# Zero products in TensorE's waits, a product moved from GpSimd to VectorE, and a new order table in the third stretch of a two-layer decoder

## The chip, the cores and the metric

The kernel runs on one core of one Trainium2 chip. The metric is the device time of one execution in microseconds (us); the median of three runs of the kernel before is 1454.74 us (1453.48 to 1459.05). An engine works through its instructions in order; semaphores make it wait for others. TensorE is PE in the rows, VectorE DVE, ScalarE ACT, GpSimd POOL, SyncE SP.

## What is computed

16 sequences of 128 tokens of width 256 go through two layers, in float32. Layer 0 is a gated state-space block, a cross attention and a mixture of 32 experts. Layer 1, the third stretch of the kernel, is

```
x = x + attn(layernorm(x))                 # causal, 16 heads of 16, with an entropy-dependent temperature
x = x + xattn(layernorm(x), ctx)           # one head of 256, plus a bias phi
x = x + ffn(layernorm(x))                  # grouped-query causal attention with rotary positions, then 2 of 8 experts

def adaptive_temperature_softmax(logits):
    p = softmax(logits)
    entropy = sum(-p * log(p + 1e-09))
    e2 = entropy * entropy
    poly = POLY[0]*e2*e2 + POLY[1]*e2*entropy + POLY[2]*e2 + POLY[3]*entropy + POLY[4]
    beta = where(entropy > 0.5, maximum(poly, 1.0), 1.0)
    return softmax(logits * beta)
```

## The kernel before

**Stretches.** Phase A (layer 0's block and cross attention and the choice of experts) ends near 338 us of the span, phase B (32 experts) near 660. `phase_c` is layer 1. It begins near 671 and ends with the tiles of the second mixture of experts (39 tiles of 128 rows, `Tiles`).

**Pairs and units.** `phase_c` works on 8 pairs (`g`) of two sequences. A pair passes through `first` (combine the results of layer 0's experts with x: `comb`; norm; transposes `t0`; projections `q`, `k`, `v`), attention `one` with the temperature, `mix` (`t1`, output projection `o`, cross attention `xk`, `xv`, `xq`, `xs`, `xtr`, `xo`), `rotary` (`t3`, `rk`, `rr`, `rq0`, `rq1`, `rv`), attention `two`, and `last` (`t5`, `o2`, `t6`, `gate`). An attention has four units (`u`: sequence and half of the heads), each of 128 x 1024 elements. For `xk` and `xv`, pairs 0 and 1 compute their context's keys and values here; the others load them.

**A unit of attention one** goes: mask and score products on TensorE (`sc`, L1466, L1468), maximum and subtraction on VectorE (`mx` L1523, `sb` L1529), exponential on ScalarE (`ex`, L1762), sum and reciprocal on VectorE (`zr`, L1779), scaling on GpSimd (`pn`, L1796), logarithm on ScalarE (`ln`, L1767), the product p log p on GpSimd (`pr`, L1799), its sum on VectorE (`hr`, L1784), the polynomial of the entropy on GpSimd (`po`, ten operations of 128 x 8, L1802 to L1817), scaling of the logits on GpSimd (`db`, L1820), second exponential on ScalarE (`e2`, L1556), eight transposes on TensorE (`tr`, L1486), copy on ScalarE (`pt`, L1559), values (`pv`, L1498), copy (`os`, L1563), two transposes (`ot`, L1504), and the division on VectorE (`out`, L1537, L1539). Attention one has one pair of score banks: the next pair's scores of unit u wait for this pair's `pt` of unit u, and the transposes of unit u + 1 wait for the next pair's `sb` of unit u.

**What sets the order.** Each engine's program is woven from generators, each of which says when its next piece is due; the due times stand in the table `AT_C`, one entry for each piece and pair, in us. The table sets only the order in which an engine's instructions are put in its queue; at run time semaphores decide when they run. The pieces of the tiles and of the routing tables (`tables_tensor`, `tables_vector`) hang on entries of it (`t5` and `wta`).

**Fetches.** `fetch0` to `fetch3` of a pair are gathers that GpSimd issues (L2309); `comb` waits for all four, and from pair 2 on, a pair's first fetch waits for `comb` two pairs before. `comb` is L1707, four instructions that read two tiles in SBUF each.

**Zero products.** `keep_warm(c, con, n, bank)` issues n products of zeros, 128 x 128 by 128 x 256, each two matmul instructions in the trace (L1085). There are ten before the third stretch's first wait and five in the first pair's `t0`, two after the second scores.

## Time and profile before

| | us |
|---|---|
| median of three runs | 1454.74 |
| lowest and highest | 1453.48, 1459.05 |
| the profiled execution | 1466.06 |
| its span | 1463.2 |
| busy in the span: TensorE, VectorE, ScalarE, GpSimd | 1312.7, 779.7, 689.0, 536.1 |
| mean granted clock of TensorE, share of full speed | 0.963 |

Shares are means over stages with different limits, so stages are read one by one. Times in rows are us from the span's start. The granted clock of a stretch is given as a share of 2.4 GHz; at 0.50 it is the lower of its two levels, 1.2 GHz. A busy TensorE is not TensorE at its peak, since matmuls overlap and their ends are modelled.

### The profile page before, as it was taken

What the parts mean: (1) busy time and instruction counts of PE and PEld (TensorE: products, weight loads), DVE (VectorE), ACT (ScalarE), POOL (GpSimd) and SP (SyncE); (2) the same over time, 40 slices, a digit from 0 to 9 for tenths busy, and PEclk for the clock granted to TensorE, in tenths of its full rate; (3) what the DMA queues carried; (4) which work ended last, traced back from release to release, by engine and by line L of the source; (5) the groups of instructions that cost most, each with busy time, mean ns of one, the idle gap of its engine ahead of it and who ended that gap; (6) DMA issues with size and microseconds to landing.
All of it is one profiled execution on the core that took longest, in us unless ns stands there. A gap on an engine that the chain in (4) does not pass through costs nothing. (4 is left out here: it accounts for less than half of the span.)

```text
span 1463.2 us, 23121 instructions
## 1 busy us (share of the span) xinstructions
PE 1312.7 (90%) x8464; PEld 989.9 (68%) x8464; DVE 779.7 (53%) x1791; ACT 689.0 (47%) x1254; POOL 536.1 (37%) x777
## 2 busy tenths in 40 slices
PE   9899999988999999896667989989989779999996
PEld 7576767757999999894334665656656545666664
DVE  4876868673111111113656687977776645433332
ACT  6454747552222222222447687768777445222221
POOL 2123130402000000006878887887867033322222
PEclk9999999999999999998869999999999989999998
DMA  9673563903877777713000001000010634322221
GB/s 352 252 200 106 123 166 106 230 12 124 292 264 264 262 267 280 279 48 98 19 1 5 20 29 33 20 29 20 0 48 16 243 97 136 60 39 41 44 39 11
DMA packets 70686, 171.00 MB, mean 117 GB/s; under 512 B 8508, under 2 KB 47425, under 8 KB 60464
## 3 DMA queue, kind: packets, MB, share of 16 engines
q1 hardware_dynamic: 54944, 144.39, 30.9%
q0 software_dynamic: 10224, 16.09, 5.3%
q10 hardware_dynamic: 5408, 9.04, 1.7%
q8 instruction: 69, 1.13, 0.3%
q14 instruction: 41, 0.34, 0.1%
HBM read 123.11 MB, written 48.07 MB: 117 GB/s over the span
## 5 line engine op out<-in xcount | busy, mean ns | idle before, releaser
L1187 ACT ACTIVATE b_ht<-ps,b_b 128x154 f32<-128x154 f32 x256 | 85.4, 387 | 205.8 <-PE ps L1154 189.5
L1202 DVE TENSOR_SCALAR b_yt<-ps,b_b 128x154 f32<-128x154 f32 x64 | 21.2, 373 | 244.0 <-PE ps L1167 244.0
L2309 POOL DMA_INDIRECT experts<-ye,gidx_all x32 | 32.1, 1002 | 325.2 <-SPq L1093 314.6
L2384 PE MATMUL ps<-experts,d_xt 128*128 x312 | 147.1, 594 | 1.2 <-ACT d_xt L2440 0.8
L1154 PE MATMUL ps<-b_xet,ring 128*128 128x154 f32 x1024 | 143.7, 298 | 3.7 <-ACT b_ht L1187 3.7
L1154 PEld LDWEIGHTS ps<-b_xet,ring 128*128 128x128 f32 x1024 | 138.3, 192 | 3.9 <-issue 3.8
L1167 PE MATMUL ps<-b_ht,ring 128*128 128x154 f32 x1024 | 139.7, 294 | 0.4 <-DVE b_yt L1202 0.4
L1167 PEld LDWEIGHTS ps<-b_ht,ring 128*128 128x128 f32 x1024 | 136.3, 189 | 0.6 <-issue 0.6
L2526 POOL DMA_INDIRECT out_dram<-d_yd,d_to x39 | 60.6, 1554 | 158.5 <-DVE d_yd L2498 151.2
L1523 DVE TENSOR_REDUCE c_mx<-ps 128x8 f32<-128x1024 f32 x64 | 77.8, 1215 | 63.8 <-PE ps L1468 63.3
L1486 PE MATMUL ps<-cf,experts 128*128 128x128 f32 x512 | 73.3, 290 | 24.8 <-DVE experts L1529 12.6
L1486 PEld LDWEIGHTS ps<-cf,experts 128*128 128x128 f32 x512 | 61.5, 149 | 37.0 <-ACT experts L1556 18.4
L2384 PEld LDWEIGHTS ps<-experts,d_xt 128*128 128x128 f32 x312 | 56.0, 190 | 41.0 <-issue 39.0
L1799 POOL TENSOR_TENSOR experts<-experts 128x1024 f32<-128x1024 f32 x32 | 75.4, 2360 | 13.3 <-ACT experts L1767 13.3
L1559 ACT ACTIVATE experts<-ps 128x1024 f32<-128x1024 f32 x64 | 65.4, 1023 | 30.7 <-PE ps L1486 26.0
L235 POOL TENSOR_SCALAR a_rs<-a_mv 128x2 f32<-128x2 f32 x24 | 6.0, 250 | 200.3 <-DVE a_mv L190 200.3
L1529 DVE TENSOR_TENSOR experts<-ps,c_mx 128x1024 f32<-128x1024 f32 x64 | 78.1, 1220 | 1.6 <-PE ps L1498 0.2
L1468 PE MATMUL ps<-experts 64*128 64x512 f32 x256 | 78.7, 694 | 0.0
L1556 ACT ACTIVATE experts<-experts 128x1024 f32<-128x1024 f32 x64 | 67.5, 1057 | 22.9 <-DVE experts L1529 13.3
L2402 PE MATMUL ps<-experts,d_gt 128*128 x312 | 73.9, 380 | 0.9 <-DVE d_gt L2479 0.9
L2447 ACT ACTIVATE d_gs<-ps 128x512 f32<-128x512 f32 x39 | 23.3, 597 | 105.4 <-PE ps L2384 102.4
L1796 POOL TENSOR_TENSOR experts<-experts,c_zz 128x1024 f32<-128x1024 f32 x32 | 60.7, 1898 | 14.3 <-DVE c_zz L1781 14.0
(336 smaller groups left out, 2839.0 us busy)
## 6 DMA issues: line engine op xcount, KB each, us to landing
ring<-in_w SPq DMA_DIRECT2D x64, 1024.0 KB, 5.4
xd<-zero SPq DMA_DIRECT2D x6, 3120.0 KB, 25.9
a_kp<-in_ctx_k SPq DMA_DIRECT2D x8, 1024.0 KB
experts<-in_wd SPq DMA_DIRECT2D x1, 7424.0 KB
d_xd<-xd SPq DMA_DIRECT2D x39, 130.0 KB, 2.1
xe<-zero SPq DMA_DIRECT2D x1, 4928.0 KB, 33.2
b_xe<-xe SPq DMA_DIRECT2D x32, 154.0 KB
ye<-b_ye ACTq DMA_DIRECT2D x32, 154.0 KB
```

The costliest lines, as they stand in the source:

```text
L1154: r = pe.matmul(ps[:, b, CAP * (m % 2):CAP * (m % 2) + CAP], w1r[:, slot, k, P * m:P * m + P], xet[:, e % 2, k, :], start=(k == 0), stop=( ...
L1167: r = pe.matmul(ps[:, 5, CAP * j:CAP * j + CAP], w2r[:, slot, m, P * j:P * j + P], ht[:, e % 2, m, :], start=(m == 0), stop=(m == MF0 - 1) ...
L1187: r = a.activation(ht[:, e % 2, m, :], ps[:, b, CAP * (m % 2):CAP * (m % 2) + CAP], ACT.Gelu, bias=b1[:, e, m:m + 1])
L1468: m = pe.matmul(ps[:, b0 + b, :], l.qt[64 * b:64 * b + 64, ch, P * s:P * s + P], l.kp[64 * b:64 * b + 64, ch, :, P * s:P * s + P], start=F ...
L1486: m = pe.transpose(ps[:, there.b0 + h // 4, P * (h % 4):P * (h % 4) + P], d[:, h, :], con["ident"])
L1523: v.tensor_reduce(l.mx[u][:, :], both, AX, ALU.max).then_inc(*c.dv.up())
L1529: v.tensor_tensor(l.d[u % l.n_d][:, :, :], both, l.mx[u][:, :, None].to_broadcast([P, NU, P]), ALU.subtract).then_inc(*l.dd.up())
L1556: a.activation(d[:, :, :], d[:, :, :], ACT.Exp).then_inc(*l.ee.up())
L1559: a.activation(d[:, :, :], l.scores(c, g, u), ACT.Copy).then_inc(*l.pt_in.up())
L1799: pool.tensor_tensor(e, e, l, ALU.mult).then_inc(*pr.up())
L2384: m = pe.matmul(ps[:, b, :], xt[:, j % 2, k, :], w13[:, bass.ds(e, 1), f:f + F1], start=(k == 0), stop=(k == KD - 1))
L2402: m = pe.matmul(ps[:, 4, 0:D], gt[:, j % 2, f, :], w2[:, bass.ds(e, 1), D * f:D * f + D], start=(f == 0), stop=(f == MF1 - 1))
```

## The change

Four things change, all in `phase_c`.

1. Zero products are issued ahead of waits: for attention one ahead of the transposes of all units of pair 0 and unit 0 of pair 1, for pair 1 ahead of `k` and `v`, for attention two ahead of the transposes of unit 2 of pair 6, for pair 7 ahead of `rq0`, and four ahead of the first count of the routing tables. They write banks that are not in use there (5, 0).
2. For pairs 0 and 1 (`BY_VECTOR = 2`) the product p log p is issued on VectorE.
3. The polynomial is computed as a product of two quadratic factors, which are found on the host: nine operations on GpSimd, with five dependent steps.
4. The table `AT_C` is another one throughout. Some of its entries (us, pairs 0 to 7):

| piece | before | after |
|---|---|---|
| fetch0 | 0, 3.8, 11.5, 20.5, 27, 146.6, 157, 202 | 0, 1.3, 11.5, 16.7, 28.4, 32.3, 86.7, 68 |
| fetch3 | 3.7, 8.8, 19.3, 25.7, 34, 158.2, 169.2, 211.7 | 5, 8.8, 19.3, 27.2, 38.7, 46.7, 98.1, 73.7 |
| xk (pairs 0, 1) | 17.2, 131.5 | 3.6, 134.8 |
| xv (pairs 0, 1) | 33.2, 136 | 6.4, 138.3 |
| xvi (pairs 0, 1) | 38.9, 137.9 | 8.3, 140.2 |
| comb | 6.4, 10.2, 20.6, 27.1, 40.1, 176.1, 193.9, 231.6 | 9.5, 12.5, 20.6, 28.6, 62.1, 50.6, 99.5, 80.3 |
| t0 | 12.5, 25.9, 79.5, 122.6, 194, 260.1, 316.6, 378 | 15.2, 27.9, 81.2, 126.2, 196.5, 261.9, 313.2, 372.4 |
| tr0 | 51.6, 86.9, 133.3, 183.6, 243.7, 305.8, 358.9, 418.6 | 48, 88.9, 127, 185.5, 245.7, 303.3, 358.3, 415.8 |
| db0 | 47.9, 81.5, 124.2, 177.2, 234.4, 295.9, 351.3, 408.2 | 44.8, 77.3, 117.9, 178.8, 237.1, 295.3, 350, 403.4 |
| t1 | 82.6, 138.7, 188.4, 244.6, 303.1, 358.4, 415.5, 462.2 | 84.4, 141, 193.1, 245.2, 305.3, 357.8, 415.3, 458 |
| tr2b | 159.6, 215.5, 267.5, 321, 385.1, 443.7, 486.3, 517.9 | 157.8, 216.2, 269.8, 327.9, 381.1, 436.1, 479.4, 517.4 |
| t3 (pair 7) | 487.9 | 485 |
| rq0 (pair 7) | 497.1 | 492.8 |
| t5 | 178.7, 238.1, 299.6, 353.7, 416, 460.1, 504.9, 527 | 179.3, 240.2, 298.3, 352.8, 411.9, 454.2, 497.2, 523.3 |

The code, without the table:

```diff
+BY_VECTOR = 2
+def quadratic_factors(p):
+    roots = sorted(np.roots([p[0], -p[1], p[2], -p[3], p[4]]), key=lambda r: (abs(r.imag), r.real))
+    return [(float(-(r + s).real), float((r * s).real)) for r, s in (roots[:2], roots[2:])]
+FACTORS = quadratic_factors(POLY)
...
         yield at("tr", u)
+        keep_warm(c, con, *warm.get((g, u), (0, 0)))
         pe.wait_ge(*l.ee.at(g, u))
...
             yield at("k")
+            if g == 1:
+                keep_warm(c, con, 4, 5)
             pe.wait_ge(*one.q_in.at(g))
...
             yield at("v")
+            if g == 1:
+                keep_warm(c, con, 5, 5)
             pe.wait_ge(*one.k_in.at(g))
...
                 v.reciprocal(zz[u][:, :], zz[u][:, :]).then_inc(*zr.up())
+                if g < BY_VECTOR:
+                    yield at("pr", u)
+                    v.wait_ge(*ln.at(g, u))
+                    v.tensor_tensor(e[:, :, :], e[:, :, :], lnp[u % 2][:, :, :], ALU.mult).then_inc(*pr.up())
                 yield at("hr", u)
...
-                yield at("pr", u)
-                pool.wait_ge(*ln.at(g, u))
-                pool.tensor_tensor(e, e, l, ALU.mult).then_inc(*pr.up())
+                if g >= BY_VECTOR:
+                    yield at("pr", u)
+                    pool.wait_ge(*ln.at(g, u))
+                    if g == BY_VECTOR and u == 0:
+                        pool.wait_ge(*pr.at(g - 1))
+                    pool.tensor_tensor(e, e, l, ALU.mult).then_inc(*pr.up())
                 yield at("po", u)
                 pool.wait_ge(*hr.at(g, u))
-                pool.tensor_tensor(sq_h, h, h, ALU.mult).then_inc(*c.po.up())
-                pool.tensor_scalar(g_h, h, -0.5, None, ALU.is_lt)
+                pool.tensor_tensor(square, h, h, ALU.mult)
+                pool.tensor_scalar(p, h, *FACTORS[0], ALU.mult, ALU.add)
+                pool.tensor_scalar(other, h, *FACTORS[1], ALU.mult, ALU.add).then_inc(*c.po.up())
+                pool.tensor_scalar(chosen, h, -0.5, POLY[0], ALU.is_lt, ALU.mult)
                 pool.wait_ge(*c.po.now())
-                pool.tensor_scalar(p, sq_h, POLY[0], POLY[2], ALU.mult, ALU.add)
-                pool.tensor_scalar(odd, sq_h, -POLY[1], -POLY[3], ALU.mult, ALU.add).then_inc(*c.po.up())
+                pool.tensor_tensor(p, p, square, ALU.add)
+                pool.tensor_tensor(other, other, square, ALU.add).then_inc(*c.po.up())
                 pool.wait_ge(*c.po.now())
-                pool.tensor_tensor(p, p, sq_h, ALU.mult)
-                pool.tensor_tensor(odd, odd, h, ALU.mult).then_inc(*c.po.up())
+                pool.tensor_tensor(p, p, other, ALU.mult).then_inc(*c.po.up())
                 pool.wait_ge(*c.po.now())
-                pool.tensor_tensor(p, p, odd, ALU.add).then_inc(*c.po.up())
-                pool.wait_ge(*c.po.now())
-                pool.tensor_scalar(p, p, POLY[4], None, ALU.add).then_inc(*c.po.up())
-                pool.wait_ge(*c.po.now())
-                pool.tensor_tensor(p, p, g_h, ALU.mult).then_inc(*c.po.up())
+                pool.tensor_tensor(p, p, chosen, ALU.mult).then_inc(*c.po.up())
                 pool.wait_ge(*c.po.now())
                 pool.tensor_scalar(p, p, 1.0, None, ALU.max).then_inc(*be.up())
...
                 if half == 0:
+                    if g == NG - 1:
+                        keep_warm(c, con, 6, 0)
                     pe.wait_ge(*two.k_in.at(g))
...
+            yield from weave([first_tensor(g), causal_tensor(c, one, con, g, tick(g), True, {(0, 0): (4, 5), (0, 1): (5, 5), (0, 2): (5, 5), (0, 3): (5, 5), (1, 0): (4, 5)}), mix_tensor(g), rotary_tensor(g),
+                              causal_tensor(c, two, con, g, tick_b(g), False, {(NG - 2, 2): (9, 0)}), last_tensor(g)])
...
                 yield settled[n] + LATE * n
+                if n == 0:
+                    keep_warm(c, con, 4, 0)
                 pe.wait_ge(*router.pr_in.at(choice))
```

## Rows read from the trace of the kernel before

**Rows 1.** Windows: span, us, busy time and count by engine, clock, DMA share, GB/s.

```profile
722.00:762.00 40.00, 26.14 (x133) 12.29 (x132) 18.82 (x25) 17.70 (x21) 32.43 (x53) 0.59 0.00 1
762.00:1160.00 398.00, 352.83 (x2587) 239.84 (x2587) 298.12 (x574) 290.54 (x468) 297.66 (x504) 0.98 0.10 34
1160.00:1198.00 38.00, 23.85 (x142) 14.43 (x142) 18.98 (x67) 11.53 (x21) 10.45 (x16) 0.78 0.53 179
1219.00:1449.00 230.00, 228.85 (x874) 141.78 (x874) 91.69 (x271) 53.60 (x128) 65.74 (x47) 1.00 0.29 51
```

**Rows 2.** Timeline of TensorE, last pair: start, us, line, tiles, count, idle before.

```profile
1217.88 0.66 PE L253 MATMUL ps<-cf,experts 128*128 128x128 f32 x4 [0.41 <-DVE experts L1539]
```

**Rows 3.** Windows, the 10 us ahead of the slow stretch.

```profile
710.00:720.00 10.00, 4.03 (x16) 2.20 (x17) 8.60 (x11) 5.54 (x8) 9.15 (x17) 1.00 0.00 0
```

**Rows 4.** Timeline of TensorE, a step at low and at full clock.

```profile
724.32 1.97 PE L1486 MATMUL ps<-cf,experts 128*128 128x128 f32 x8 [2.22 <-ACT experts L1556]
729.37 2.04 PE L1468 MATMUL ps<-experts 64*128 64x512 f32 x4
...
768.55 1.04 PE L1486 MATMUL ps<-cf,experts 128*128 128x128 f32 x8
...
773.76 1.13 PE L1468 MATMUL ps<-experts 64*128 64x512 f32 x4
```

**Rows 5.** Chain of waits, pair 7's first transposes of mix.

```profile
1145.74 0.59 PE ps L253 x4
```

**Rows 6.** Timelines, zero products and start of the third stretch.

```profile
660.13 2.32 PE L1085 MATMUL ps<-zero 128*128 128x256 f32 x10
671.07 9.46 PE L1085 MATMUL ps<-zero 128*128 128x256 f32 x30 [8.61 <-PEq L1093]
680.89 0.66 PE L253 MATMUL ps<-cf,experts 128*128 128x128 f32 x4 [0.36 <-ACT experts L226]
682.24 1.99 PE L272 MATMUL ps<-c_xt_f,weights 128*128 128x256 f32 x8 [0.69 <-ACT c_xt_f L262]
...
671.55 1.80 DVE L1707 SCALAR_TENSOR_TENSOR x_all<-experts,gwt_all,x_all 128x256 f32<-128x256 f32 x4
```

**Rows 7.** Timeline of GpSimd, product and polynomial of one unit.

```profile
731.32 2.35 POOL L1799 TENSOR_TENSOR experts<-experts 128x1024 f32<-128x1024 f32 x1
733.62 0.21 POOL L1802 TENSOR_TENSOR c_sq_h<-c_en 128x8 f32<-128x8 f32 x1
...
736.31 1.90 POOL L1820 TENSOR_TENSOR experts<-experts,c_po 128x1024 f32<-128x1024 f32 x1
```

**Rows 8.** Timelines, a combine beside GpSimd, and the combines' durations in ns.

```profile
698.93 1.91 DVE L1707 SCALAR_TENSOR_TENSOR x_all<-experts,gwt_all,x_all 128x256 f32<-128x256 f32 x1
...
698.31 0.95 POOL L2309 DMA_INDIRECT experts<-ye,gidx_all  x1 [0.30 <-issue]
699.28 1.27 POOL L1749 TENSOR_TENSOR x_all<-x_all,weights 128x512 f32<-128x512 f32 x1
...
L1707 DVE SCALAR_TENSOR_TENSOR x_all<-experts,gwt_all,x_all x32: 472/479/1911, 671.5 to 915.7; 128x256 f32<-128x256 f32 x32
```

**Rows 9.** Timeline of VectorE, a subtraction of 1024 columns.

```profile
733.04 1.21 DVE L1529 TENSOR_TENSOR experts<-ps,c_mx 128x1024 f32<-128x1024 f32 x1
```

**Rows 10.** Waits between 775 and 1146: us, times, longest.

```profile
ACT experts L1556 <- POOL experts L1820: 8.6, 11, 1.7
```

**Rows 11.** Timelines of the last pairs, TensorE and ScalarE.

```profile
1174.00 1.97 PE L1486 MATMUL ps<-cf,experts 128*128 128x128 f32 x8 [5.55 <-ACT experts L1556]
1175.98 1.12 PE L253 MATMUL ps<-cf,c_x_rms 128*128 128x128 f32 x4
...
1188.25 3.78 PE L272 MATMUL ps<-c_xt_r,weights 128*128 128x256 f32 x8 [3.37 <-ACT experts L1574]
...
1185.77 2.42 ACT L1574 ACTIVATE experts<-ps,cf 128x512 f32<-128x512 f32 x4 [2.45 <-PE ps L1968]
```

**Rows 12.** Windows, behind the first zero products.

```profile
680.00:690.00 10.00, 6.90 (x31) 4.94 (x29) 1.57 (x6) 5.13 (x10) 8.71 (x11) 1.00 0.16 43
```

More of the change, by code:

```diff
@@ L1297 @@
 AT_C = {
[87 rows of a table removed]
-    "xadd": (185.7, 244.3, 305.3, 362.1, 425.5, 465.6, 510.8, 531.1), "rtp": (187, 245.6, 306.6, 363.4, 433, 467.3, 513.6, 532.4),
[3 rows of a table removed]
-    "count": (None, 254.6, None, 374.9, None, 476.6, 522.3, 539.6), "gap": (None, 255, None, 372.8, None, 476.7, 522.3, 539.6),
-    "wta": (None, 257.5, None, 376.3, None, 478.1, 522.8, 540.1), "weights": (None, 259.1, None, 379.9, None, 485.5, 524.1, 541.4),
[4 rows of a table removed]
[87 rows of a table added]
+    "xadd": (185, 245.3, 307.4, 359.5, 416.8, 461.5, 501.3, 527.4), "rtp": (186.3, 246.6, 306.4, 358.5, 420.4, 463.2, 502.6, 528.7),
[3 rows of a table added]
+    "gap": (None, 256.3, None, 368.3, None, 472.6, 511.3, 535.8), "count": (None, 256.3, None, 367.5, None, 472.4, 514.1, 535.8),
+    "wta": (None, 259.2, None, 369.9, None, 474, 518.5, 536.3), "weights": (None, 260.8, None, 371.5, None, 481.4, 519.8, 537.6),
[4 rows of a table added]
 }
@@ L1441, in earlier, with causal_tensor @@
     return tally.at(n, j)
-def causal_tensor(c, l, con, g, at, woven):
+def causal_tensor(c, l, con, g, at, woven, warm):
     pe, ps = c.nc.tensor, c.ps
@@ L1608, in phase_c @@
         zz, en, po = ([sb("%s%d" % (name, u), [P, NU]) for u in range(len(UNITS))] for name in ("zz", "en", "po"))
-        gt = [[sb("%s%d" % (name, u), [P, NU]) for name in ("sq_h", "g_h", "odd")] for u in range(len(UNITS))]
+        gt = [[sb("%s%d" % (name, u), [P, NU]) for name in ("square", "other", "chosen")] for u in range(len(UNITS))]
         x_rot, x_rms = [sb("x_rot%d" % n, [P, GS, D]) for n in range(2)], sb("x_rms", [P, GS, D])
@@ L1792, in unit @@
                 e, l, d = ent[u % 2][:, :, :], lnp[u % 2][:, :, :], one.d[u][:, :, :]
-                h, p, (sq_h, g_h, odd) = en[u][:, :], po[u][:, :], (x[:, :] for x in gt[u])
+                h, p, (square, other, chosen) = en[u][:, :], po[u][:, :], (x[:, :] for x in gt[u])
                 yield at("pn", u)
@@ L2161, in tensor_program @@
         def tensor_program(g):
-            yield from weave([first_tensor(g), causal_tensor(c, one, con, g, tick(g), True), mix_tensor(g), rotary_tensor(g),
-                              causal_tensor(c, two, con, g, tick_b(g), False), last_tensor(g)])
+            yield from weave([first_tensor(g), causal_tensor(c, one, con, g, tick(g), True, {(0, 0): (4, 5), (0, 1): (5, 5), (0, 2): (5, 5), (0, 3): (5, 5), (1, 0): (4, 5)}), mix_tensor(g), rotary_tensor(g),
+                              causal_tensor(c, two, con, g, tick_b(g), False, {(NG - 2, 2): (9, 0)}), last_tensor(g)])
         def vector_program(g):
```

188 rows, old and new, of the table AT_C are left out of this document.

## The prediction

> **What bounds the kernel now.** I read the stages first: mean load and granted clock of four stretches [rows 1]. TensorE is busy 229 of 230 us in the last one, where the experts' tiles run back to back, and no edit lies there: it only shifts with the moment at which the last pair's transposes (L253, 1217.88) start [rows 2]. Before that, the reader is to look at the granted clock. It is 0.98 for 398 us in the middle, 0.59 in 722 to 762 (TensorE busy 26 of 40 us) and 0.78 in 1160 to 1198. The slice 710 to 720 says what went ahead: TensorE was busy 4.0 of 10 us, still at clock 1.00, and the clock fell behind it [rows 3]. The level in such a stretch is 1.2 GHz instead of 2.4, and it doubles TensorE's steps: eight transposes take 1.97 us where they take 1.04 at full clock, the score products 2.04 and 1.13 [rows 4].
>
> Then I laid the trace beside the kernel's own due times, as marks along the program, not as prices. The first unit's transposes (`tr0`, pair 0, due 51.6) start at 724.32, so the origin is 672.7; `tr0` of pair 1 (86.9) starts at 768.55 [rows 4], origin 681.7: 9.0 us lost. `t1` of pair 7 (462.2) starts at 1145.74 [rows 5], origin 683.5: only 1.9 us more in 377. `t5` of pair 7 (527.0) at 1217.88 [rows 2], origin 690.9: 7.4 more. So the loss lies where the clock is low, and there the change puts its zero products.
>
> **The change part by part.**
>
> *Start, by hand from rows.* The new order puts `xk`, `xv` and `xvi` ahead of `comb` of pair 0 on TensorE, ScalarE and VectorE. Now VectorE combines pair 0 at 671.55, and TensorE turns it at 680.89 after 30 zero instructions that began at 671.07 [rows 6]. In the new order TensorE first runs its ten zero products (20 instructions; two thirds of the 9.46 us of 30, to about 678), then `xk` 1.99 (the form's row), its bias on ScalarE (two pieces, by half of L1574's four in 2.42: 1.2), `xv` 1.99, `xvi` (half of a 1024-wide VectorE operation of 1.2: 0.6), so `comb` starts at about 683.7, 12 us late. Today pair 0 waits on from 673.4 for GpSimd, which has fetches queued; that slack goes, so `t0` comes near 689.8, 9 us late. Queued behind: GpSimd's first fetch of pair 2 waits for `comb` of pair 0, and with it fetches of pairs 3 to 5. Much is absorbed: pair 0's units are stretched today by GpSimd (products 2.35 us each on it [rows 7]), and four of these go to VectorE. Following both orders row by row I reach `db0` of pair 0 at about 721 in both. But TensorE has the zero products: four ahead of `k`, five ahead of `v`, four ahead of `tr0`. One product is two instructions, and ten instructions took 2.32 us at full clock, 0.46 us per product [rows 6]; at half the clock I double it. Thirteen are 6.0 us, of which some 4 fit in waits. So `tr0` comes 2.0 us **late** (726.3). Bounds: 0 to +9 (nothing absorbed).
>
> *The pairs 0 and 1, from 724.32 to 768.55.* 44.2 us today, four steps. What full clock gives back in a step: 0.93 (transposes), 0.91 (scores), and about half as much again for the mask's and the values' products, which also run in a step (an estimate): 2.6, four times, some 10 us, all between TensorE's wait and VectorE's next, of which 9.0 showed as loss. The zero products (five per step, 2.3 us) sit in front of the transposes, in the wait for VectorE's maximum and subtraction (two of 1.2 us), and are hidden there at full clock; four ahead of `tr0` of pair 1 are not, TensorE being dense in 762 and on: +1.0 after some slack. Against it, the new order has three more combines and twelve fetches in these pairs (1.80 us each for a combine, 0.95 for a fetch on GpSimd [rows 6, 8]), and its own due times make the distance 40.9 where the old made it 35.3. If the clock is held: 44.2 to 40.9 is −3.3; +1.0 for the zeros.
>
> *The product on VectorE.* No row has this operation on VectorE. Nearest are its 1024-wide subtraction and sums, 1.2 us [rows 9]; I take 1.2, bounds 1.2 and 3.1. The upper bound is from the combine, which reads two tiles in SBUF: a piece takes 0.48 us, but the one that began at 698.93 lasted to 700.84 (1.91), and GpSimd's two-input addition ran from 699.28 to 700.55 [rows 8]. A 1.9 us GpSimd operation can hold a product as long. Eight products leave GpSimd (8 × 2.36); +0.8 on the path for one or two collisions. The page "SBUF — State Buffer" of the Trainium skill, section "Who interferes with whom", says it as a rule: a VectorE instruction with two SBUF inputs and a GpSimd one that reads SBUF exclude each other, the later one waiting for the whole of the other. The trace agrees, and the rule speaks against this move: if each of the eight products met half of a scaling, it would give 7.6 us of collisions in place of 0.8, and this part +5 in place of −1.5. So for this part −3.3 + 1.0 + 0.8 = **−1.5** (bounds −9 and +6).
>
> *The polynomial.* Today 2.69 us from L1802 (733.62) to the scaling (736.31), ten small operations in seven dependent steps [rows 7]. New: nine in five. By the same spacings (0.17 independent, 0.29 per dependent step) 2.23: 0.46 less for every unit. It counts where GpSimd is last before ScalarE's second exponential: 11 times between 775 and 1146 [rows 10]. 11 × 0.46 is **−5.0** for the middle. Bounds: 0 (TensorE, 353 of 398 us busy there, takes it back) and −11 (all 24 units). The later fetches and combines that left the middle are counted in it; the due times give −6.2.
>
> *Last pairs.* Three waits carry the loss: 5.55 us ahead of the transposes at 1174.00 (then 1.97), ScalarE's keys 1185.77 to 1188.2 while TensorE stands 3.37, then `rq0` 3.78 us where its form takes 1.99 at full clock [rows 6, 11]. The nine zero products (4.2 us) ahead of `tr2b` of pair 6 fill the first, four ahead of the counts the wait before it, six (2.8 us) ahead of `rq0` the last, 0.5 over the 2.4 us of keys. With clock, `rq0` gives 1.8. The new order puts `t3`, `rk`, `rr` nearer: 12.3 us today from 1175.98 to 1188.25, 7.8 by the new marks plus 0.8 for zeros: −3.7. `t3` itself waits for VectorE, which now does a subtraction first, +0.5; the rest of the pair is 0.6 longer by its marks. Sum −1.8 − 3.7 + 0.5 + 0.5 = **−4.5** (bounds −8 and 0).
>
> Sum: +2.0 − 1.5 − 5.0 − 4.5 = **−9.0 us**, from a span of 1463.2 to 1454. The profiled execution took 1466.06 with what lies around its span, 11 us over the median of the runs (1454.74); I take the difference over unchanged: **1446 us**.
>
> **Rivals.**
> *A, forecast*: clock held in most waits, 1441 to 1450; 0.42.
> *B, clock held throughout.* All 16.4 us of origin drift in the two slow stretches go but 3, and the middle gives its 5: 1454.7 − 13 − 5 = 1437. For it: the drift lies so squarely there. Against: the loaded start, and waits such as those behind pair 1 that get no zeros. 0.20.
> *C, no net change.* The start and collisions eat the early gain and the middle is TensorE's: +2 + 1.5 − 1.5 − 4.5, about 1452. For it: TensorE 353 of 398 in the middle. 0.30. That includes the case that zero products do not lift the clock; but in 680 to 690, behind the zero stretch, the clock was 1.00 with TensorE busy 6.9 of 10 us [rows 12], which speaks against.
> *D, slower.* The zero products meet the clock already low, which the late start makes likely (VectorE's chain leaves TensorE waiting 3 to 4 us before `sc3`). At 1.2 GHz five take about 4.6 us in a wait of 2.4, +2 in each of four steps; the thirteen ahead of `k`, `v`, `tr0` take 5 more, those ahead of `tr0` of pair 1 one more. +2 + 8 + 5 + 1 − 5.0 − 4.5 is about +7, 1462; it decides once fewer than half of the early waits run at full clock. Against: a low clock ends behind dense work. 0.08.
>
> **How the numbers follow.** A measurement tells 0.5% (7.3 us) from no change. Faster by more (below 1447.5): most of A and B, 0.55. Within: part of A and C, 0.37. Slower: D, 0.08. The range leaves out some of B's and D's far ends: 1437 to 1456.
>
> **What would show it.** Granted clock in the 40 us behind the first transposes: near 1.0 for A and B, 0.6 for D. `comb` of pair 0 starting near 684 and `t0` near 690 show the start; `tr0` of pair 0 near 726 its absorption. VectorE's product at 1.2 us, or up to 3.1 where GpSimd runs. The chain from L1802's successor to the scaling 2.2 us. Clock 1.00 around the end's transposes and `rq0` 2 us long. From the last `t5` to the end 245 us as now. I am wrong if the first transposes come before 722 or behind 731, if the middle (`tr0` of pair 1 to `t1` of pair 7, 377 us) does not shrink, or if the early clock stays at 0.6.

## The result: no gain, and where the expected one went

The changed kernel takes 1464.22 us (median of 18 runs, 1458.34 to 1470.05), the kernel before 1460.47 beside it (18 runs, 1453.48 to 1464.72): ratio 1.0033, 95% interval 1.0020 to 1.0046. A later set of runs has it at 0.9994 (0.9969 to 1.0019). It is the same within the 0.5% that a measurement can tell; the forecast was 1446 us, 0.6% below before, with a range of 1437 to 1456.

A warning for all that follows: the median of the kernel before moved between sets of runs, from 1459.3 to 1469.7 us, and single profiled executions of one kernel differ by 3 to 8 us. So I compare ratios and times within a set and name the set; ratios of different sets are compared only with this in mind. Traces serve for where time goes, not for how much.

The same windows of the kernel after as in [rows 1], and then the 20 us behind its start, in this execution and in a second one of the same kernel (columns as there: busy time of TensorE, weight load, VectorE, ScalarE, GpSimd, then the granted clock):

```profile
722.00:762.00 40.00, 28.20 (x173) 17.30 (x173) 29.83 (x43) 19.08 (x24) 35.92 (x60) 0.87 0.07 20
762.00:1160.00 398.00, 353.27 (x2596) 242.27 (x2628) 302.70 (x584) 291.01 (x470) 281.24 (x463) 0.97 0.10 34
1160.00:1198.00 38.00, 32.32 (x177) 22.78 (x178) 19.16 (x59) 13.57 (x27) 12.62 (x19) 0.87 0.46 151
1219.00:1449.00 230.00, 228.31 (x875) 141.70 (x874) 92.08 (x271) 52.46 (x127) 65.01 (x46) 1.00 0.28 50
684.00:704.00 20.00, 13.60 (x43) 8.67 (x44) 10.29 (x26) 5.68 (x10) 15.24 (x22) 0.83 0.16 47
```

```profile
684.00:704.00 20.00, 12.34 (x32) 8.00 (x30) 7.80 (x21) 4.60 (x9) 11.52 (x16) 0.66 0.16 47
722.00:762.00 40.00, 31.30 (x168) 20.55 (x167) 32.71 (x42) 19.18 (x23) 33.41 (x56) 0.87 0.07 20
```

The zero products did lift the clock: 0.87 in 722 to 762 instead of 0.59. What they did not do is save time there. TensorE's timeline of after gives the marks that answer to [rows 2, 4, 5]:

```profile
671.61 6.68 PE L1095 MATMUL ps<-zero 128*128 128x256 f32 x20 [8.70 <-PEq L1103]
...
726.42 0.82 PE L1497 MATMUL ps<-cf,experts 128*128 128x128 f32 x6
...
770.98 1.89 PE L1095 MATMUL ps<-zero 128*128 128x256 f32 x8
772.70 1.04 PE L1497 MATMUL ps<-cf,experts 128*128 128x128 f32 x8
...
1142.49 0.66 PE L263 MATMUL ps<-cf,experts 128*128 128x128 f32 x4
...
1216.71 0.66 PE L263 MATMUL ps<-cf,experts 128*128 128x128 f32 x4 [0.41 <-DVE experts L1550]
```

The first transposes of pair 0 come at 726.42 (I had 726.3), those of pair 1 at 772.70 where before had 768.55. From these rows, and the same four marks in every later kernel, I divide the stretch into four parts: *start* (first zero product of the third stretch to `tr0` of pair 0), *pairs 0 and 1* (to `tr0` of pair 1), *middle* (to `t1` of pair 7) and *end* (to `t5` of pair 7). All in us, one profiled execution each:

| kernel | start | pairs 0 and 1 | middle | end |
|---|---|---|---|---|
| before | 53.2 | 44.2 | 377.2 | 72.1 |
| after | 54.8 | 46.3 | 369.8 | 74.2 |
| after, second execution | 62.1 | 45.6 | 370.7 | 71.7 |
| old order, all other edits | 55.1 | 35.6 | 374.6 | 72.8 |
| the same, second execution | 55.4 | 35.6 | 371.9 | 69.5 |

The third and fourth line are the answer in short, and the experiments below lead to it. Line numbers: the changed file is 10 to 24 lines longer there, so L1497 is the transposes, L1570 their copy, L1567 the second exponential, L1822 or L1801 the product (GpSimd or VectorE), L1840 the scaling of the logits, L1722 the combine, L2333 a fetch, L1585 the keys, L282 and L291 projections, L1095 zero products.

### The profile page after: what moved, and what is told of

The parts are those of the page before. It is cut to its first block and busy times, and to the rows that moved or that the text cites. A ratio compares the mean times of both kernels' runs of the same rounds, so it can differ in the third digit from the quotient of the medians.

```text
span 1462.0 us, 23254 instructions
## 1 busy us (share of the span) xinstructions
PE 1322.7 (90%) x8526; PEld 1004.7 (69%) x8566; DVE 789.5 (54%) x1799; ACT 688.7 (47%) x1254; POOL 517.8 (35%) x737
## 5 line engine op out<-in xcount | busy, mean ns | idle before, releaser
L2333 POOL DMA_INDIRECT experts<-ye,gidx_all x32 | 33.6, 1049 | 330.7 <-SPq L1103 312.7
L1497 PE MATMUL ps<-cf,experts 128*128 128x128 f32 x512 | 70.3, 283 | 11.7 <-DVE experts L1540 7.9
L1567 ACT ACTIVATE experts<-experts 128x1024 f32<-128x1024 f32 x64 | 67.3, 1054 | 28.8 <-POOL experts L1840 16.2
L1540 DVE TENSOR_TENSOR experts<-ps,c_mx 128x1024 f32<-128x1024 f32 x64 | 78.1, 1222 | 1.8
L1497 PEld LDWEIGHTS ps<-cf,experts 128*128 128x128 f32 x512 | 59.2, 145 | 24.9 <-issue 13.1
L1570 ACT ACTIVATE experts<-ps 128x1024 f32<-128x1024 f32 x64 | 65.1, 1022 | 23.5 <-PE ps L1497 23.1
L1840 POOL TENSOR_TENSOR experts<-experts,c_po 128x1024 f32<-128x1024 f32 x32 | 61.8, 1930 | 1.5
## 6 DMA issues: line engine op xcount, KB each, us to landing
xd<-zero SPq DMA_DIRECT2D x6, 3120.0 KB, 25.7
```

What stands on the lines that cost most here:

```text
L1497: m = pe.transpose(ps[:, there.b0 + h // 4, P * (h % 4):P * (h % 4) + P], d[:, h, :], con["ident"])
L1540: v.tensor_tensor(l.d[u % l.n_d][:, :, :], both, l.mx[u][:, :, None].to_broadcast([P, NU, P]), ALU.subtract).then_inc(*l.dd.up())
L1567: a.activation(d[:, :, :], d[:, :, :], ACT.Exp).then_inc(*l.ee.up())
L1570: a.activation(d[:, :, :], l.scores(c, g, u), ACT.Copy).then_inc(*l.pt_in.up())
L1840: pool.tensor_tensor(d, d, wide(po[u]), ALU.mult).then_inc(*db.up())
```

## The experiments

### One part taken out of the kernel after

These ran in one set, with before at 1468.44 us; after itself is not in it. First the zero products:

```diff
-            if g == 1:
-                keep_warm(c, con, 4, 5)
...
-            if g == 1:
-                keep_warm(c, con, 5, 5)
...
-                    if g == NG - 1:
-                        keep_warm(c, con, 6, 0)
...
-True, {(0, 0): (4, 5), (0, 1): (5, 5), (0, 2): (5, 5), (0, 3): (5, 5), (1, 0): (4, 5)})
+True, {})
-False, {(NG - 2, 2): (9, 0)})
+False, {})
...
-                if n == 0:
-                    keep_warm(c, con, 4, 0)
```

> The kernel after without any of the added zero products (order table, products on VectorE and new polynomial stay). Theory 'the zeros are in the way' (in the trace of after, four stand 1.9 us straight ahead of the transposes of pair 1, six run on for 2.4 us behind ScalarE's keys in the last pair, and in pairs 0 and 1 the waits that the clock was to shorten are on GpSimd and ScalarE): 1460 to 1463, within 4 us below after's 1464.2, the first transposes of pair 0 about 1.3 us earlier, and the clock near 0.6 again in 722 to 762. Rival 'the zeros carry what is gained, the table loses it': the low clock returns with its 9 us of drift in pairs 0 and 1 and its 6 at the end, 1470 to 1476.

1468.74 us, ratio 1.0010 (0.9981 to 1.0039): not to be told from after's 1.0033 and 0.9994. In its trace TensorE's clock in 722 to 762 is back at 0.59, and the four parts are 57.5, 47.2, 369.9, 75.0:

```profile
722.00:762.00 40.00, 22.78 (x110) 12.99 (x112) 30.44 (x40) 18.74 (x22) 32.38 (x54) 0.59 0.06 17
```

So in this order a clock of 0.87 or of 0.59 makes about 1 us of difference in pairs 0 and 1 (47.2 against 46.3 and 45.6). Neither theory is borne out: the first transposes come no earlier (727.3 us, after a start of 57.5), and the 9 us of drift do not come back either. Then the product back on GpSimd:

```diff
-BY_VECTOR = 2
+BY_VECTOR = 0
```

> The kernel after with the product p log p of pairs 0 and 1 back on GpSimd. Theory 'port': each product on VectorE stretches a GpSimd operation beside it by 1.0 us or so and lies in VectorE's chain, so it gives little; back on GpSimd it costs 8 times 2.36 us there, of which one per step is on the chain to the second exponential: +1 to +4 against after, 1465 to 1468. Rival 'the product on VectorE is what lost the early time': -2 to -5, 1459 to 1462, with the distance from the first transposes of pair 0 to those of pair 1 back from 46.3 to 44 us.

1477.28 us, 1.0065 (1.0036 to 1.0095), so 5 to 10 us more than after, whose ratios are from two other sets: the product on VectorE helps in this order. Pairs 0 and 1 take 53.0 us instead of 46.3, which says what bounds them. GpSimd's groups in 720 to 780 of that kernel (count, busy, mean ns, idle before):

```profile
L1822 POOL TENSOR_TENSOR experts<-experts 128x1024 f32<-128x1024 f32 x6 | 14.1, 2354 | 0.0
L1840 POOL TENSOR_TENSOR experts<-experts,c_po 128x1024 f32<-128x1024 f32 x6 | 11.4, 1895 | 0.3
L1816 POOL TENSOR_TENSOR experts<-experts,c_zz 128x1024 f32<-128x1024 f32 x5 | 9.5, 1899 | 0.0
L2333 POOL DMA_INDIRECT experts<-ye,gidx_all x8 | 8.0, 997 | 1.7 <-issue 1.6
```

Hardly any of these groups waited for another engine: in this kernel GpSimd is what the rest waits for. Eight of its instructions in 60 us are fetches, and the old order has none there. Then the order:

```diff
-    "tr0": (48, 88.9, 127, 185.5, 245.7, 303.3, 358.3, 415.8)
+    "tr0": (51.6, 86.9, 133.3, 183.6, 243.7, 305.8, 358.9, 418.6)
...
```

(and so all entries, as in before)

> The kernel after with the order table of the kernel before (zero products, products on VectorE and new polynomial stay). Theory 'the table lost it': in the trace of after VectorE waits 4.2 us for the gather of pair 6 ahead of pair 2's work (combine at 785), ScalarE takes exponential and logarithm ahead of a copy for 3 us, and 12 us of context projections stand ahead of pair 0; with the old order the first transposes come at 724 and pair 3's first maximum near 826 instead of 838: 1455 to 1459, faster than both. Rival 'the zeros lost it': 1462 to 1466, as after.

1452.01 us, **0.9904** (0.9867 to 0.9942): 14 us less than before by the ratio (16 by the medians), 17 less than no_zeros in the same set, faster than both kernels. A later set gave 0.9902 (0.9878 to 0.9926). The table was what ate the gain. Its window of 722 to 762, and TensorE's four steps:

```profile
722.00:762.00 40.00, 33.29 (x214) 22.68 (x215) 31.77 (x43) 26.44 (x34) 27.27 (x55) 1.00 0.00 1
```

```profile
726.84 1.09 PE L1497 MATMUL ps<-cf,experts 128*128 128x128 f32 x8
...
731.49 2.32 PE L1095 MATMUL ps<-zero 128*128 128x256 f32 x10
734.27 1.06 PE L1497 MATMUL ps<-cf,experts 128*128 128x128 f32 x8 [0.46 <-DVE experts L1540]
...
741.68 1.06 PE L1497 MATMUL ps<-cf,experts 128*128 128x128 f32 x8 [0.46 <-DVE experts L1540]
...
748.78 1.06 PE L1497 MATMUL ps<-cf,experts 128*128 128x128 f32 x8
```

A step is 7.4 us where before had 10 (724.32, 734.4, 744.3); the zeros end just as the transposes may begin. In after the same four stand at 726.4, 735.0, 745.9 and 758.1. Its longest stand in these steps is for ScalarE's copy (L1570), which is queued behind a second exponential that waits for GpSimd's scaling:

```profile
750.83 0.97 PE L1509 MATMUL ps<-experts 128*32 128x128 f32 x16 [3.85 <-ACT experts L1570]
...
746.83 1.06 ACT L1567 ACTIVATE experts<-experts 128x1024 f32<-128x1024 f32 x1 [5.05 <-POOL experts L1840]
```

Last, the polynomial by itself in the kernel before:

```diff
-                pool.tensor_tensor(sq_h, h, h, ALU.mult).then_inc(*c.po.up())
-                pool.tensor_scalar(g_h, h, -0.5, None, ALU.is_lt)
...
+                pool.tensor_tensor(square, h, h, ALU.mult)
+                pool.tensor_scalar(p, h, *FACTORS[0], ALU.mult, ALU.add)
...
```

> The kernel before with the new polynomial alone. The trace of after has 2.47 us for it where before had 2.69, 0.22 less, not the 0.46 predicted; where GpSimd is last, 11 times in the middle and some 6 times in pairs 0 and 1: -2 to -4 against before. Rival 'TensorE takes it all back': 0, within 1 us of before.

1466.77 us, 0.9995 (0.9970 to 1.0020): nothing to be seen, the rival. Its middle takes 376.6 us, before's 377.2. What it saves itself is small too; GpSimd in after:

```profile
742.43 0.20 POOL L1825 TENSOR_TENSOR c_square<-c_en 128x8 f32<-128x8 f32 x1
742.70 0.20 POOL L1826 TENSOR_SCALAR c_po<-c_en 128x8 f32<-128x8 f32 x1
742.96 0.20 POOL L1827 TENSOR_SCALAR c_other<-c_en 128x8 f32<-128x8 f32 x1
743.23 0.26 POOL L1828 TENSOR_SCALAR c_chosen<-c_en 128x8 f32<-128x8 f32 x1
...
744.57 0.25 POOL L1837 TENSOR_SCALAR c_po<-c_po 128x8 f32<-128x8 f32 x1
744.90 1.90 POOL L1840 TENSOR_TENSOR experts<-experts,c_po 128x1024 f32<-128x1024 f32 x1
```

744.90 − 742.43 is 2.47, against 2.69 in [rows 7]: 0.22 less, not 0.46.

### Which parts of the order

A set with before at 1469.73. Its reference is the kernel after, unchanged:

> The kernel after itself, beside the next three on the same chip, so that they are compared within one set of runs. Expected: ratio to before between 1.000 and 1.006, as measured.

1468.24 us, 0.9994. Then only the fetches and combines that moved:

```diff
-"fetch0": (..., 28.4, 32.3, 86.7, 68)  "comb": (..., 62.1, 50.6, 99.5, 80.3)
+"fetch0": (..., 27, 146.6, 157, 202)   "comb": (..., 40.1, 176.1, 193.9, 231.6)
...
```

Likewise `fetch1` to `fetch3`, and the norm of pair 5 behind its combine (`n0s` and `n0p` at 187 and 196).

> The kernel after with the fetches and combines of pairs 4 to 7 (and the norm of pair 5 behind its combine) back at the old due times; zeros, products, polynomial and the rest of the new table stay. Theory 'GpSimd is the bound of pairs 0 and 1, and the twelve fetches moved there lie on it' (with the product on GpSimd as well the same order lost another 14 us in the trace): 8 to 12 us less than after, ratio to before 0.992 to 0.996, first transposes of pair 1 at 763 to 766 instead of 772.7. Rival 'it is the twelve microseconds of context work at the start, or the rest of the order': within 3 us of after, transposes of pair 1 at 771 to 773.

1464.81 us, 0.9970 (0.9946 to 0.9993): 3.4 us less than after, where I expected 8 to 12. So the fetches on GpSimd are a part of the loss and not its bulk. In the trace (against the second execution of after), pairs 0 and 1 fell from 45.6 to 42.2 and the three steps behind them from 34.2 to 27.9. In the first execution of after VectorE stood 4.20 us for the last fetch of pair 6, which GpSimd had issued only at 782.45, with pair 2's sums and maximum queued behind it, and TensorE stood after that:

```profile
785.37 3.44 DVE L1722 SCALAR_TENSOR_TENSOR x_all<-experts,gwt_all,x_all 128x256 f32<-128x256 f32 x4 [4.20 <-DMA experts<-ye,gidx_all]
```

```profile
797.43 1.94 PE L1497 MATMUL ps<-cf,experts 128*128 128x128 f32 x8 [3.24 <-DVE experts L1540]
```

Then the context projections back behind pair 0's own:

```diff
-"xk": (3.6, ...)  "xki": (5.5, ...)   "xv": (6.4, ...)   "xvi": (8.3, ...)
+"xk": (20.3, ...) "xki": (24.8, ...)  "xv": (36.3, ...)  "xvi": (42, ...)
```

> The kernel after with the context projections xk and xv of pair 0 and their copies back behind pair 0's projections; all else stays. Theory 'GpSimd': t0 of pair 0 comes 8 us earlier, but the first transposes of pair 1 at most 3 us earlier, since the fetches still lie on GpSimd: ratio to before 0.999 to 1.003. Rival 'the start': all of it comes through, 7 to 9 us less than after, ratio 0.995 to 0.998.

1460.28 us, 0.9940 (0.9914 to 0.9965): 8 us less than after. By the times the rival holds: all of it comes through. The traces tell less of where: this kernel's start is 51.6 us, against 54.8 and 62.1 in after, but its pairs 0 and 1 take 49.0, against 46.3 and 45.6. With the fetches still in place, pairs 0 and 1 took some of it back, as the other theory had it. The start is also where two executions of one kernel part. In after's first profile TensorE reaches the first scores at 699.07, in its second at 704.47, because there the projections met the clock at its low level (1.2 GHz):

```profile
691.60 1.11 PE L263 MATMUL ps<-cf,experts 128*128 128x128 f32 x4 [1.38 <-ACT experts L236]
693.40 3.78 PE L282 MATMUL ps<-c_xt_f,weights 128*128 128x256 f32 x8 [0.69 <-ACT c_xt_f L272]
697.87 3.78 PE L282 MATMUL ps<-c_xt_f,weights 128*128 128x256 f32 x8 [0.69 <-ACT experts L1746]
```

In the first execution each of these L282 groups took 1.99 us. And the zero products by themselves, in the kernel before; against the old order with all edits that is

```diff
-BY_VECTOR = 2
+BY_VECTOR = 0
...
-                pool.tensor_tensor(square, h, h, ALU.mult)
+                pool.tensor_tensor(sq_h, h, h, ALU.mult).then_inc(*c.po.up())
...
```

> The kernel before with the added zero products alone (old order, product on GpSimd, old polynomial). Beside the kernel with the old order and all three edits (ratio 0.990) it tells what the zeros bring and what the product brings. Theory 'the clock is held only where TensorE is the one waited for, and the old order's pairs 0 and 1 wait for GpSimd too': zeros alone give 2 to 4 us, ratio 0.997 to 0.999, and the product on VectorE the other 6 us or so. Rival 'it is the clock': zeros alone give 8 to 12 us, ratio 0.991 to 0.994, and the product nothing.

1460.93 us, 0.9938 (0.9909 to 0.9968): 8.8 us, and pairs 0 and 1 take 36.4 us instead of 44.2. Its start is 50.2 us (53.2 before); its middle is 382.5 (377.2 before), so in this one profile the stretch behind took some 5 us back. With the product still on GpSimd, which is then busy 37.09 of 40 us, the steps are as short as with it on VectorE:

```profile
722.00:762.00 40.00, 33.25 (x229) 22.17 (x230) 23.77 (x37) 26.82 (x35) 37.09 (x62) 1.00 0.00 1
```

So in the old order the clock is what pairs 0 and 1 wait for, and a GpSimd that is busy 93% of the time does not keep the gain away. The new order puts six fetches (0.95 to 1.83 us each, and up to 0.30 of issue) between the first transposes of pairs 0 and 1, where the old one has none, and places the rest of the work otherwise; there the clock buys little. The fetches by themselves account for the 3.4 us above.

### Both parts, and the edits with the old order

A set with before at 1459.28. First the two table edits above (fetches and combines, context projections) in one kernel:

> The kernel after with both parts of the old order at once: context projections of pair 0 behind pair 0's projections, and fetches and combines of pairs 4 to 7 late. Alone they gave ratios of 0.994 and 0.997 to before, where after has about 1.002. Theory 'two queues, two losses, additive': 0.989 to 0.992, as with the whole old order (0.990). Rival 'the same chain is late by either': 0.993 to 0.996.

1458.51 us, 0.9989 (0.9974 to 1.0003); 0.9974 (0.9962 to 0.9986) in another set. Both expectations fail: the ratio lies above both of their ranges, and above what start_old alone had in its set (0.9940), although the times are alike (1458.51 and 1456.92 against 1460.28): what moved between the sets is the kernel before. In the trace the start is 51.6 us; pairs 0 and 1 are at 42.9 us, not 35.6, although GpSimd is busy only 31.55 of 40 us and has no fetch there. So the fetches are not the bulk of what the new order loses in these pairs. Then the old order with product and polynomial, and the zero products gone as in the first diff:

> The kernel before with the product of pairs 0 and 1 on VectorE and the new polynomial, without the added zero products. Theory 'product and clock are independent': the product is worth 0.3% (zeros alone gave 0.994, all three 0.990): 0.996 to 0.998. Rival 'the product helps only with the clock held' (its steps wait for TensorE at half clock otherwise): 0.999 to 1.001.

1457.85 us, 0.9979 (0.9960 to 0.9997): product and polynomial without clock are worth at most 6 us, likely some 3. Pairs 0 and 1: 44.2 us, as before to a tenth; the middle is 369.7. Only the early zero products, again in the old order:

```diff
-False, {(NG - 2, 2): (9, 0)})
+False, {})
...
-                        keep_warm(c, con, 6, 0)
...
-                    keep_warm(c, con, 4, 0)
```

> The old order with product, polynomial and only the zero products of pairs 0 and 1; those at the end (four, nine and six) are gone. In the trace of the kernel with all of them in the old order, the last pairs took 72.8 us from t1 of pair 7 to t5, 72.1 in before, so the end's zeros brought nothing: theory: as with all of them, 0.989 to 0.992. Rival 'they return 3 to 5 us': 0.993 to 0.995.

1448.87 us, 0.9911 (0.9890 to 0.9932): 9.0 us less than without any, in the same set. The early zero products are the gain; those at the end bring nothing to be seen. This kernel is the one to keep. And fewer in place of none, with the four ahead of pair 1's first transposes gone:

```diff
-                        keep_warm(c, con, 6, 0)
+                        keep_warm(c, con, 3, 0)
...
-(0, 3): (5, 5), (1, 0): (4, 5)}
+(0, 3): (5, 5)}
```

> The old order with all edits, but three zero products ahead of rq0 instead of six, and none ahead of the first transposes of pair 1, where the old-order trace has 1.9 us of them straight ahead of the transposes. In that trace twelve zero instructions ahead of rq0 last from 1177.68 to 1182.06, 1.9 us behind ScalarE's keys. Theory 'what stands directly on TensorE's path is paid in full': 2 to 4 us less than with all, 0.987 to 0.989. Rival 'the clock falls again without them': 0.991 to 0.993.

1449.51 us, 0.9923 (0.9905 to 0.9941), not to be told from the last; it falls into the rival's range, and the 2 to 4 us of the theory are not seen. The traces tell more of the place. Six ahead of `rq0`, in after, with ScalarE's keys:

```profile
1181.99 4.08 PE L1095 MATMUL ps<-zero 128*128 128x256 f32 x12
1185.91 1.89 PE L282 MATMUL ps<-c_xt_r,weights 128*128 128x256 f32 x8
...
1181.09 2.42 ACT L1585 ACTIVATE experts<-ps,cf 128x512 f32<-128x512 f32 x4 [0.98 <-PE ps L1988]
```

none, with the old order:

```profile
1174.66 3.63 PE L282 MATMUL ps<-c_xt_r,weights 128*128 128x256 f32 x8 [2.51 <-ACT experts L1585]
```

and three:

```profile
1169.93 1.56 PE L1095 MATMUL ps<-zero 128*128 128x256 f32 x6
1172.51 1.99 PE L282 MATMUL ps<-c_xt_r,weights 128*128 128x256 f32 x8 [1.02 <-ACT experts L1585]
```

Six run 2.4 us past the keys (1183.5 to 1185.9), for 1.9 us that `rq0` gives back. Three end ahead of the keys and `rq0` is short as well. The end takes 72.8 and 69.5 us with six, 69.7 with none, 68.1 with three, so no difference by number is shown.

### The table cut in two

A set with before at 1466.77. Its reference once more:

> The old order with all three other edits once more, as reference for the next three: ratio to before 0.988 to 0.994.

1451.45 us, 0.9902. The old order up to 100 us and the new one behind, with the fetches and combines of pairs 5 to 7 late:

```diff
-    "tr0": (48, 88.9, 127, 185.5, 245.7, 303.3, 358.3, 415.8)
+    "tr0": (51.6, 86.9, 127, 185.5, 245.7, 303.3, 358.3, 415.8)
...
```

> All edits, with the old order for every piece that it has due before 100 us (start, pairs 0 and 1), and for the fetches and combines of pairs 5 to 7; the new order for the rest. Theory 'the loss lies in the first 100 us': as the old order, within 2 us, 0.989 to 0.993. Rival 'the new order loses behind it as well': 0.995 to 0.999.

1458.96 us, 0.9941 (0.9919 to 0.9963). Pairs 0 and 1 take 35.6 us again, the middle 379.8 instead of 371.9. After itself has 369.8 and 370.7 there with nearly the same entries, so what this kernel loses behind may come from the seam between the two tables; no run separates that. The reverse:

```diff
-    "tr0": (48, 88.9, 127, 185.5, 245.7, 303.3, 358.3, 415.8)
+    "tr0": (48, 88.9, 133.3, 183.6, 243.7, 305.8, 358.9, 418.6)
...
```

> All edits, with the new order for every piece that it has due before 100 us (fetches and combines of all pairs among them), and the old order for the rest. Theory 'the loss lies in the first 100 us': 0.999 to 1.003, as after. Rival: 0.990 to 0.995.

1471.39 us, 1.0037 (1.0013 to 1.0061); pairs 0 and 1 take 48.6 us, the start 62.2. So the first 100 us of the new table are enough for all of its loss: 20 us against the reference in this set. The rest alone costs 7.5 us. The two do not add up (after is 13 to 19 us above the old order by the ratios), so the 7.5 are no share of after's loss. The rival of the first, that it loses behind as well, holds in kind (0.9941 lies just below where I had put it). And the old polynomial in the old order, the other edits in:

```diff
-                pool.tensor_tensor(square, h, h, ALU.mult)
+                pool.tensor_tensor(sq_h, h, h, ALU.mult).then_inc(*c.po.up())
...
```

> The old order with zero products and products on VectorE, and the old polynomial. Alone the new polynomial gave nothing (0.9995). Theory 'TensorE takes it back': within 2 us of the old order with all edits. Rival 'with the clock held GpSimd is last more often': 3 to 5 us more than with all edits, 0.993 to 0.996.

1456.29 us, 0.9922 (0.9897 to 0.9946): 4.8 us more by the medians, 2.9 by the ratios, and the intervals overlap. Its middle is 375.8 us, in the two kernels with the new one 374.6 and 371.9. It stays open whether the polynomial gives 0 or 5 us once the clock is held.

### One place on ScalarE

With start and fetches put back, the trace shows ScalarE going through a second exponential that waits for GpSimd, an exponential and a logarithm, ahead of the copy (L1570) that TensorE needs:

```profile
740.49 1.06 ACT L1567 ACTIVATE experts<-experts 128x1024 f32<-128x1024 f32 x1 [4.56 <-POOL experts L1840]
741.46 1.04 ACT L1777 ACTIVATE experts<-experts 128x1024 f32<-128x1024 f32 x1
742.40 1.13 ACT L1782 ACTIVATE experts<-experts,c_tiny 128x1024 f32<-128x1024 f32 x1
743.44 1.00 ACT L1570 ACTIVATE experts<-ps 128x1024 f32<-128x1024 f32 x1
```

```profile
744.49 1.08 PE L1509 MATMUL ps<-experts 128*32 128x128 f32 x16 [3.70 <-ACT experts L1570]
```

It looked like the whole rest of the loss, so I exchanged just these instructions (before at 1461.33):

```diff
-"ex1": (33.1, 67.2, ...)   "pt2": (69.5, ...)
+"ex1": (33.1, 66, ...)     "pt2": (66.05, ...)
```

> The kernel with start and late fetches of the old order once more, as reference for the next: 0.995 to 1.000 of before.

1456.92 us, 0.9974.

> As the reference, but on ScalarE the copy of the turned unit 2 of pair 0 stands ahead of the second exponential of unit 3 and of the logarithm of pair 1's unit 0, as in the old order; the three other engines' orders are the same. Theory 'this is the rest of the loss': the wait of 3.7 us ahead of the value products near 744 falls to 1.1, the step from 12.5 to 8 or 9 us, 3 to 6 us off in all. Rival 'the exponential is then late, and the wait only moves to the next transposes': within 1.5 us of the reference.

1456.67 us, 0.9987 (0.9968 to 1.0006): the same. The copy now begins at 741.01, 0.16 us behind the transposes, and TensorE's wait is 1.11. But the reference's own profile, another execution of the same code, has this wait at 1.88, not 3.70: the stall was one execution's. A conspicuous row in one profile was no cause. What the rest of the new order costs in the first 100 us (42 to 44 us where the old one has 35.6) is not settled. The traces show TensorE waiting for VectorE's subtraction (L1540) up to 3.1 us a step there, and up to 0.46 in the old order; no run changed that.

## Why the prediction was wrong, point by point

Four terms made the forecast of −9.0 us. Against the profile of before they measured as follows, in the two executions of after (from the table above; each figure has the scatter of a single profile):

| term | forecast | first | second |
|---|---|---|---|
| start | +2.0 | +1.6 | +8.9 |
| pairs 0 and 1 | −1.5 | +2.1 | +1.4 |
| middle | −5.0 | −7.4 | −6.5 |
| last pairs | −4.5 | +2.1 | −0.4 |

- **What bounds the kernel.** Right for the kernel before: the low clock in 722 to 762 cost what the drift of the due times said, 9.0 us. Zero products alone, in the old order, returned 7.8 us in pairs 0 and 1, and 8.8 in all (its start was shorter as well, its middle longer). With the clock held the distance is 35.6 us, and the old due times said 35.3.
- **Start, +2.0.** The steps were right in the trace: `comb` at 683.7 (forecast 683.7), `t0` at 690.2 (689.8), first transposes at 726.4 (726.3). The term was still mis-sized, and the agreement of the first execution was luck. The second has 734.4, behind the 731 that I had named as a sign of being wrong. The other kernels with this start have 57.5 (no zero products), 61.8 (product on GpSimd), 63.2 (fetches late) and 62.2 us (new order early) where before has 53.2, and taking the context projections away from the front gave 8 us in the runs. "Much is absorbed" held for one placing of the clock's low stretches. The bound of +9 that I had written beside it was the better number.
- **Pairs 0 and 1, −1.5.** This step failed. I read the new order's 40.9 us off its due times and took it as reached once the clock was held. It is not: 46.3 and 45.6 us with the clock at 0.87, and 47.2 without zero products at 0.59. The due times held for the old order (35.3 due, 35.6 measured) and not for the new. I also counted the change from 44.2 to the new marks, not what the zero products would give with the old ones, and so never saw that edit 4 threw away 10 us of edit 1. Of these 10 us, the fetches on GpSimd are some 3.4. I had written twelve fetches; by the table only six are due between 48 and 88.9, and the trace has six there. GpSimd was busy 32.43 of 40 us already [rows 1] and is busy 35.92 now. With the fetches and the context projections both put back, pairs 0 and 1 still take 42 to 44 us. What costs the rest stays open.
- **The product on VectorE, +0.8.** Its duration was right (1.2 us, up to 2.65). Its sign was not asked properly: in the new order it saves 5 to 10 us, by taking 2.35 us a unit from an engine that is then the one waited for. In the old order with the clock held its gain is small: 0.9922 with product and zero products against 0.9938 with zero products alone, in two sets and with intervals that overlap. The price of collisions fell mostly on GpSimd:

```profile
758.12 2.75 POOL L1840 TENSOR_TENSOR experts<-experts,c_po 128x1024 f32<-128x1024 f32 x1
...
757.91 1.21 DVE L1801 TENSOR_TENSOR experts<-experts 128x1024 f32<-128x1024 f32 x1
```

  The scaling takes 1.90 us elsewhere; begun 0.21 us behind VectorE's product, it takes 2.75. That agrees with the rule of the Trainium skill (page "SBUF — State Buffer", section "Who interferes with whom") that issue order decides who waits: in the kernel with the old order a product that began at 720.78, while GpSimd scaled from 720.45 to 722.35, took 2.65 us itself. The row that I had taken as agreement does not show who waits: in [rows 8] the combine began 0.35 us ahead of the addition and was itself the one stretched; a fetch was then still running on GpSimd. By that rule taken alone I had put this part at +5; no run shows such a cost.
- **The polynomial, −5.0.** Mis-sized twice. It is 0.22 us a unit instead of 0.46: the four independent operations at its head stand 0.27, 0.26 and 0.27 apart, where I had taken 0.17 (and by the spacings that I named the sum is 0.41, not 0.46). And alone it moved nothing (0.9995), as its bound of 0 said; that TensorE takes it back is the likely reason, not a shown one. The middle did shrink, by 7.4 and 6.5 us, so the term came out near its number by luck. The traces put this shrinking beside another edit. With the product on VectorE the middle is 369.7 against 376.6 (old order, new polynomial, no zero products), 375.8 against 382.5 (old order, old polynomial, zero products), and 369.8 or 370.7 against 373.7 (new order). With the new polynomial it is 376.6 against 377.2, and 374.6 or 371.9 against 375.8. Two profiled middles of one kernel differ by 2.7 us (374.6 and 371.9), so only the product's 7 us stand out, and I had booked nothing for it behind pair 1's first transposes.
- **Last pairs, −4.5.** This step failed as well; by size it missed as much as any (+2.1 and −0.4 measured). `rq0` is 1.89 us as forecast, but six zero products run 2.4 us past ScalarE's keys, where I had allowed 0.5; their first part ran at half clock, which doubles them. And the nearer marks of `t3`, `rk` and `rr` did not come: from `t3` to `rq0` it takes 12.2 us (1173.68 to 1185.91) where I had 8.6 and before 12.3. The granted clock of 1160 to 1198 is 0.87, not 1.00, and the steps between are at the low level, nine zero products before them or not:

```profile
1173.68 0.66 PE L263 MATMUL ps<-cf,c_x_rms 128*128 128x128 f32 x4 [1.87 <-ACT c_x_rms L2046]
...
1177.13 1.92 PE L1497 MATMUL ps<-cf,experts 128*128 128x128 f32 x8
1178.98 2.07 PE L1988 MATMUL ps<-c_kr,weights 64*128 64x256 f32 x4
```

  In the second execution, where the window's clock is 0.96, the same distance is 9.4 us.
- **The rivals.** C's outcome is what happened ("start and collisions eat the early gain"): the start did, but collisions are not what the runs show for the rest; it was the order, in part its fetches on GpSimd. D's mechanism did not happen: in 722 to 762 two of the three groups of five zero products took 2.32 us, as at full clock, and one 3.11. The time lies 8.2 us above the range; 5.7 of them are the base, 1454.74 in the first three runs and 1460.47 in eighteen. As ratios the range was 0.988 to 1.001, and the two sets gave 1.0033 and 0.9994.

## What to carry to other kernels

Price each edit of a bundle against the kernel with the others undone, above all an order table: here three edits were worth 14 us, and the fourth took them all. A distance between due times is a forecast of the order's author, not a measurement; it held for the order that had been measured before and not for the new one. A full engine is no proof that a clock gain is lost: with GpSimd busy 37.09 of 40 us it came through, and with GpSimd at 31.55 in the new order most of it did not. And zero products ahead of a wait should end before it does: five in 2.32 us at full clock did so in the old order's early steps, six begun at half clock ran 2.4 us over. Where the clock may be low when they begin, count them at half clock.

## What the runs showed of the hardware

- Where the low-clock stretches of TensorE fall differs between executions of the same code: 684 to 704 had a granted clock of 0.83 in one and 0.66 in another, and the first transposes stood at 726.4 and 734.4 us; 5.4 of these 8 us are there at the first scores (699.07 and 704.47). With the context projections first the start cost 8 us in the runs, though the two take 1.99 us each on TensorE.
- Zero products held the clock in the old order: 1.00 over 722 to 762 in the profiles of four kernels with that order throughout (zero products alone, all edits, only the early ones, the old polynomial), and 0.96 with the four ahead of pair 1's first transposes gone, where it was 0.59 without; TensorE was busy 32 to 34 of 40 us, zeros included.
- A two-input VectorE operation and a two-input GpSimd one that overlap cost whichever began later, small ones too: GpSimd's 128 x 2 operation of 0.72 us took 1.74 at 775.94, and its 128 x 8 of 0.20 took 1.11 at 724.76 (old order, all edits), beside VectorE's product.
